# A six-layer decoder on one core: feed-forward rounding on GpSimd, maxima by four heads in one pass, gate products as scalar_tensor_tensor, new orders of work

## The reference

```python
x = _layernorm(x + _L0_attn_ref(x, Wq, Wk, Wv))                  # 16 heads of 16
x = _layernorm(x + _L0_xattn_ref(x, ctx, ctx, ...))              # 77 keys, biases
x = _layernorm(x + _L0_ffn_ref(x, w_gate, w_up, w_down))         # see below
x = _layernorm(x + _L1_attn_ref(x, qkv_w, ...))                  # rotary q and k
x = _layernorm(x + _L1_xattn_ref(ctx, x))                        # alignment by dynamic programming
x = _layernorm(x + _L1_ffn_ref(x, ...))                          # attention whose output is gated
```

## Time and profile before

| | us |
|---|---|
| median of three runs (6032.72 to 6035.66) | 6035.6 |
| the profiled execution | 6025.65 |
| its span, first to last instruction | 6023.9 |
| PE busy | 5378.2 (89%) |
| DVE busy | 4989.1 (83%) |
| ACT busy | 4263.0 (71%) |
| POOL busy | 2542.2 (42%) |

### The profile page before, as it was taken

How to read it: one execution, slowest core, us unless ns; L and a number is a source line. 1 busy time by engine, 2 the same in 40 slices (tenths; PEclk the granted TensorE clock), 3 DMA queues, 4 the chain that set the end, 5 groups by cost and what they waited for, 6 DMA issues and landing times. The chain is left out here.

```text
span 6023.9 us, 139116 instructions
## 1 busy us (share of the span) xinstructions
PE 5378.2 (89%) x54914; PEld 3756.3 (62%) x54914; DVE 4989.1 (83%) x11551; ACT 4263.0 (71%) x8049; POOL 2542.2 (42%) x2574
## 2 busy tenths in 40 slices
PE   6999999969999999977999999999309999999998
PEld 4666666646666666655777767767206666666666
DVE  6888888869999999986777777777678888888887
ACT  5777777758888888875666666666326777777776
POOL 0112111223333333333444444444107777777775
PEclk9999999989999999999999999999659999999999
DMA  1111111110000000001010010010100000000000
GB/s 53 49 43 45 47 43 49 40 32 29 30 29 26 30 30 30 25 24 34 29 33 29 29 33 29 29 33 29 39 26 18 26 30 26 30 26 30 26 30 22
DMA packets 140663, 193.91 MB, mean 32 GB/s; under 512 B 26353, under 2 KB 63985, under 8 KB 139633
## 3 DMA queue, kind: packets, MB, share of 16 engines
q1 hardware_dynamic: 140016, 185.00, 9.8%
HBM read 112.77 MB, written 72.18 MB: 31 GB/s over the span
## 5 line engine op out<-in xcount | busy, mean ns | idle before, releaser
L1193 DVE TENSOR_REDUCE Cmp<-pj 128x2 f32<-128x512 f32 x1024 | 635.7, 684 | 145.7 <-PE pj L874 145.6
L1193 DVE TENSOR_REDUCE Dmp<-pj 128x2 f32<-128x512 f32 x1024 | 649.0, 681 | 84.2 <-PE pj L874 84.0
L1013 ACT ACTIVATE Cpr<-pj 128x512 f32<-128x512 f32 x1024 | 528.9, 604 | 221.8 <-PE pj L807 221.8
L1193 DVE TENSOR_REDUCE Amp<-pj 128x2 f32<-128x512 f32 x1024 | 629.5, 682 | 65.0 <-PE pj L874 65.0
L1013 ACT ACTIVATE Apr<-pj 128x512 f32<-128x512 f32 x1024 | 522.0, 615 | 191.9 <-PE pj L807 191.9
L1013 ACT ACTIVATE Dpr<-pj 128x512 f32<-128x512 f32 x1024 | 526.5, 599 | 185.5 <-PE pj L807 185.4
L1127 POOL TENSOR_SCALAR Ave<-Amv 128x2 f32<-128x2 f32 x64 | 14.6, 228 | 976.9 <-DVE Amv L1261 976.9
L1127 POOL TENSOR_SCALAR Bve<-Bmv 128x2 f32<-128x2 f32 x128 | 29.2, 228 | 874.5 <-DVE Bmv L1261 874.5
L1099 POOL TENSOR_TENSOR Dnrm<-Dnrm,power 128x32 f32<-128x32 f32 x64 | 348.7, 5449 | 51.2 <-DVE Dnrm L1171 51.2
L807 PE MATMUL pj<-Dq,Dk 32*128 32x256 f32 x4096 | 332.8, 403 | 0.2 <-ACT Dpr L1013 0.2
L807 PE MATMUL pj<-Aq,Ak 32*128 32x256 f32 x4096 | 328.0, 396 | 2.1 <-DVE Aq L1200 1.2
(11 more groups left out here) (305 smaller groups left out, 14980.6 us busy)
## 6 DMA issues: line engine op xcount, KB each, us to landing
Ax0T<-in_xT SPq DMA_DIRECT2D x64, 256.0 KB, 2.9
Ax<-in_x SPq DMA_DIRECT2D x64, 256.0 KB, 3.1
x_A_scratch<-Ax SPq DMA_DIRECT2D x64, 256.0 KB, 2.0
Bx<-x_A_scratch SPq DMA_DIRECT2D x64, 256.0 KB, 2.9
x_B_scratch<-Bx SPq DMA_DIRECT2D x64, 256.0 KB, 2.0
Cx<-x_B_scratch SPq DMA_DIRECT2D x64, 256.0 KB, 2.8
x_C_scratch<-Cqr SPq DMA_DIRECT2D x64, 256.0 KB, 2.0
Dx<-x_C_scratch SPq DMA_DIRECT2D x64, 256.0 KB
```

Source lines behind the costliest of these rows:

```text
L1013: ck.tell(act.activation(dst, ck.bank(step + (bank,))[0:n, :], ACT.Exp, scale=HD ** -0.5), "probs_ready", step)
L1193: ins = dve.tensor_reduce(dst, src, AX.X, ALU.max, negate=True)
```

## The change

Five things change in the code, and with them the orders. `GROUPS` is 4 in A and B and stays 3 in C and D. A3's value bias is added by DVE when it writes the values, and ACT no longer copies them nor adds the bias behind the attention. A `max` step of pass C takes four heads, one in each row group, and four banks; the steps become half as many. The feed-forward input is rounded by POOL, with DVE keeping the scales. The gate products are all scalar_tensor_tensor, the first of them two instructions where it was one, with the factor 2 x 3 moved to another product.

```diff
-GROUPS = 3
+GROUPS = {"A": 4, "B": 4, "C": 3, "D": 3}
-VALUE_BIASES = ("A3_bv", "A4_bv")
+VALUE_BIASES = ("A4_bv",)
+VALUES_BY_ACT = ("A4",)
+ROW_GROUPS = {"A1": 2, "A2": 2, "A3": 4, "A4": 2}
 def max_heads(att, i):
+    n = ROW_GROUPS[att]
+    i, part = divmod(i, 4 // n)
+    groups = range(n * part, n * part + n)
     if tiles_of(att) == 2:
-        c, e, pair = i // 4, i % 4 // 2, i % 2
-        return [[8 * c + 2 * g + e] for g in (2 * pair, 2 * pair + 1)]
+        c, e = divmod(i, 2)
+        return [[8 * c + 2 * g + e] for g in groups]
...
-                        for i in range(2):
+                        for i in range(len(heads)):
                             ck.wait_bank_free(step + (i,))
                         for hh in range(len(heads[0])):
                             for t in range(QT):
-                                for i in range(2):
+                                for i in range(len(heads)):
...
+                    elif kind == "fq":          # gpsimd
+                        ck.wait("scales_ready", step)
+                        for t in range(QT):
+                            ins = pool.tensor_scalar(xq_f[s][:, t], x[s][:, t], qsc[s][:, t, 3:4], MAGIC, ALU.mult, ALU.add)
+                        link(ck, ins)
+                        ck.tell(pool.tensor_scalar(xq[s][:], xq_f[s][:], MAGIC, QMAX, ALU.subtract, ALU.min), "xq_ready", step)
...
-                        link(ck, dve.reciprocal(qsc[s][:, :, 2:3], qsc[s][:, :, 1:2]))
-                        link(ck, dve.tensor_scalar(qsc[s][:, :, 3:4], qsc[s][:, :, 2:3], QMAX, None, ALU.mult))
-                        for t in range(QT):
-                            ins = dve.tensor_scalar(xq_f[s][:, t], x[s][:, t], qsc[s][:, t, 3:4], MAGIC, ALU.mult, ALU.add)
-                        link(ck, ins)
-                        link(ck, dve.tensor_scalar(xq[s][:], xq_f[s][:], MAGIC, QMAX, ALU.subtract, ALU.min))
+                        dve.reciprocal(qsc[s][:, :, 2:3], qsc[s][:, :, 1:2])
...
-                        dve.tensor_tensor(gs[s][:, 7:9, :], ex[s][:, :, nr:H + 1].rearrange("p t i -> p i t"),
-                                          gs[s][:, 6:7, :].to_broadcast([P, 2, QT]), ALU.mult)
-                        link(ck, dve.tensor_tensor(gs[s][:, 9, :], gs[s][:, 4, :], gs[s][:, 5, :], ALU.mult))
-                        dve.tensor_tensor(gs[s][:, 10, :], gs[s][:, 7, :], gs[s][:, 8, :], ALU.add)
+                        for i in range(2):
+                            dve.scalar_tensor_tensor(out=gs[s][:, 7 + i, :], in0=ex[s][:, :, nr + i], scalar=1.0,
+                                                     in1=gs[s][:, 6, :], op0=ALU.mult, op1=ALU.mult)
+                        link(ck, dve.scalar_tensor_tensor(out=gs[s][:, 9, :], in0=gs[s][:, 4, :], scalar=2.0 * ROUTED,
+                                                          in1=gs[s][:, 5, :], op0=ALU.mult, op1=ALU.mult))
+                        dve.scalar_tensor_tensor(out=gs[s][:, 10, :], in0=gs[s][:, 7, :], scalar=1.0, in1=gs[s][:, 8, :],
+                                                 op0=ALU.mult, op1=ALU.add)
```

More of the change, by code:

```diff
@@ L128, in before_core @@
     if att == "A1":
-        steps = steps[:2] + maxima(att, b, 0)[:2] + steps[2:] + maxima(att, b, 0)[2:]
+        half = max_steps(att) // 4
+        steps = steps[:2] + maxima(att, b, 0)[:half] + steps[2:] + maxima(att, b, 0)[half:]
     else:
@@ L146, in core @@
     if tiles_of(att) == 2:
-        return p[:1] + second[:2] + p[1:2] + second[2:] + shifted + p[2:3] + first + p[3:] + last
+        return p[:1] + second[:len(second) // 2] + p[1:2] + second[len(second) // 2:] + shifted + p[2:3] + first + p[3:] + last
     return p[:1] + second + shifted + p[1:] + first + last
@@ L200 @@
         "sp": (
-            526, 0, 209,
+            309, 526, 0,
         ),
@@ L278, in bank_uses @@
     if kind == "max":
-        return [step + (0,), step + (1,)]
+        return [step + (g,) for g in range(ROW_GROUPS[step[1]])]
     if kind == "gu":
@@ L296, in signals @@
             "xqT": ["xqT_ready"], "gu": ["tanh_ready"], "hq": ["hid_rounded", "hq_ready"], "hT": ["hqT_ready"],
[L297 removed]
+            "mix": ["exps_ready"], "v": ["v_ready"] * (att in VALUES_BY_ACT),
         },
         "dve": {
[L300 removed]
+            "q": ["q_tokens"] * (att in ("A3", "A4")), "k": ["q_tokens"] * (att == "A3"), "v": ["v_ready"] * (att not in VALUES_BY_ACT),
             "rot": ["dve_step", "k_rotated"] if att == "A3" else ["norms2"],
[L302 removed]
+            "max": ["max_done"] * ROW_GROUPS.get(att, 0), "shift": ["q_shifted"] * 2,
             "norm": ["dve_step", "normed"] + ["x_used"] * (att == "A1" and step[-1] == 1),
             "oproj": ["proj_taken"], "path": ["dve_step", "path_ready"], "expand": ["x4_used"],
[L305 removed]
+            "down": ["down_taken"], "ln": ["dve_step", "var_ready"], "fq": ["dve_step"] * 3 + ["scales_ready"],
             "gu": ["gated", "hid_ready"], "hq": ["dve_step"] * 3 + ["scale_ready"], "dist": ["dist_ready"],
@@ L349, with __init__ @@
 class Counts:
-    def __init__(self, lines):
+    def __init__(self, lines, groups):
         self.at, self.total, self.bank, self.banks = {}, {x: 0 for x in SIGNALS}, {}, [0] * BANKS
@@ L371, in __init__ @@
             if step[0] == "core":
-                self.group[step] = len(cores) % GROUPS
-                if len(cores) >= GROUPS:
-                    _, att, b, p = cores[-GROUPS]
+                self.group[step] = len(cores) % groups
+                if len(cores) >= groups:
+                    _, att, b, p = cores[-groups]
                     self.freed_by[step] = ("pv", att, b, octet_of(att, p))
@@ L556, in __init__ @@
                 self.ve, self.rstd = each("ve", [P, QT, 2]), each("rstd", [P, QT, 2])
-                self.pr = [[sb(f"{phase}pr{i}_{g}", [P, QT, S], F32, where) for g in range(4)] for i in range(GROUPS)]
+                self.pr = [[sb(f"{phase}pr{i}_{g}", [P, QT, S], F32, where) for g in range(4)] for i in range(GROUPS[phase])]
                 if phase == "A":
@@ L1021, in do @@
                         ck.tell(ins, "out_taken", step)
-                    elif kind == "v" and att in ("A3", "A4"):
+                    elif kind == "v" and att in VALUES_BY_ACT:
                         ck.wait_bank_full(step)
@@ L1172, in do @@
                                   "norms2", step)
-                    elif kind == "v" and att in ("A1", "A2"):
+                    elif kind == "v" and att not in VALUES_BY_ACT:
                         ck.wait_bank_full(step)
@@ L1337, in do @@
                                                           in1=gs[s][:, 10, :], op0=ALU.mult, op1=ALU.mult))
-                        ck.tell(dve.tensor_tensor(gs[s][:, 15, :], gs[s][:, 11, :], gs[s][:, 12, :], ALU.add), "mixed", step)
+                        ck.tell(dve.scalar_tensor_tensor(out=gs[s][:, 15, :], in0=gs[s][:, 11, :], scalar=1.0, in1=gs[s][:, 12, :],
+                                                         op0=ALU.mult, op1=ALU.add), "mixed", step)
                 walk(dve, "dve", do)
@@ L1390, in _ @@
                                                                          in1=out3[:], op0=ALU.mult, op1=ALU.add))
-                counts = Counts(lines)
+                counts = Counts(lines, GROUPS[phase])
                 with ExitStack() as blocks:
```

62 lines of the change are left out of this document (31 added, 31 removed).

## The result

The changed kernel takes 5862.9 us at the median of four runs (5853.6 to 5864.4); the kernel before 6034.2 (6029.7 to 6035.7). The ratio is 0.9714, 95% interval 0.9697 to 0.9731: 171 us faster. The forecast was 5782, its range 5700 to 5890; the time lies in the range, but 81 us above the forecast and outside the likeliest case's own range of 5710 to 5850. The profiled execution has a span of 5862.6 us.

A forecast was written before the change was run, and what follows sets the result against it. DVE was taken to bound pass B, PE passes A, C and D. Terms 26 + 64 + 90 + 74 = 254 us off 6025.65 gave 5772, set at 5782 against the runs' median; range 5700 to 5890.

The forecast's parts named there:

- likeliest case: Whole kernel: the forecast of 5782 us holds, own range 5710 to 5850, chance 0.71.
- mechanism of B: Pass B: DVE is the bound, so moving the rounding to POOL takes 1.0 us off the period, 64 us in all.
- The operation that the trace did not show: Pass B: POOL's 128x512 tensor_scalar with bf16 out, rounding the feed-forward input, taken as 2.4 us.
- rival 3: Pass B: POOL's rounding, layernorm, store, load and PE's keys close a ring; kernel slower, 6089 us at z = 9; chance 0.03.
- the values' bank: Pass A: PE needs this bank one score step later, when DVE's copy is done; 0.4 us a sequence, 26 us.
- the wait at maxima 7: Pass A: PE's wait before the second half of maxima 7, 0.5 us a sequence, stays because DVE's order there is unchanged.
- I take 1.4 of the 2.5: Pass C: the new order removes 1.4 of 2.5 us of PE stall a period, 90 us in all.
- the next limit: Pass C: with banks free in time, DVE, at some 20 us of work and links, becomes what limits the period.
- rival 1: Passes A and C: the new orders give nothing, DVE being late in C; 5898 us, chance 0.14.
- I take it as free of the wait: Pass D: gate products as scalar_tensor_tensor do not wait for POOL's port; 1.0 us less 0.1 for the extra instruction.
- Rival 2: Pass D: the port holds scalar_tensor_tensor too, so the 0.9 us is lost; 5840 us, chance 0.08.
- takes both off the way: Pass D: moving gate products and path clears the way from maxima 2 to the shift; part of 1.15 us, 74 us.

## Why the prediction was right, and where it was not

**Direction, mechanism of B, untouched parts: right.** B was held by DVE, and its period fell by 1.19 us where 1.0 was taken (DVE's rows of `fq` were 1.12 and the links 0.1). The operation that the trace did not show, bounded by 1.2 and 5.45 us and taken as 2.4, cost 1.93; the two half-size ones, taken at 1.23 from the earlier trace rows, cost 0.48. The ring of rival 3 never came near: PE's wait for the load ahead of its keys was 0.5 us in the whole stretch. The alignment took 191 us, 190 before.

**A (26 us forecast, none got).** The steps given were right: the values' bank came free in time, the wait at maxima 7 stayed, the fourth group was free, and the median fell by 0.35 us where 0.4 was taken. That size was in part luck: the reason given was the values' bank alone, and without the layernorm's move only 0.12 us came. What failed is the part never priced: the layernorm behind the shift moves GpSimd's layernorm, SP's store and the load queued behind it, and a load that had just been in time was not. The prediction followed that chain for B only, as rival 3. Its price, 27 us in A and 27 in D (from the first to the last start of the table's instruction, 63 periods: 1131 to 1104 and 1402 to 1375 us with the stores moved), is 54 of the 81 us that were missed.

**C (90 us forecast, 42 got): the term was mis-sized, and not by its stalls.** "I take 1.4 of the 2.5": the order took 2.0 off score steps and maxima, more than that. But 1.2 of it came back in the steps that now stand elsewhere, shifts, transpositions and projections, and only 0.8 was kept; the "little over half" left no room for so much. Nor was DVE "the next limit": relieved of the values' copy (0.64 us of its 18.3 us busy a period) it changed nothing. The same run rules out rival 1's reason, DVE. That the maxima as such gain little was right.

**D (74 us forecast, 42 got; from first to last start 46, and 73 with the later stores): with those the sum comes out, by a wrong step and so by luck.** "I take it as free of the wait" is false. The evidence was L1233, 481 ns beside GpSimd's power function of 5.45 us; what it showed was that the power function did not hold it up, not that the form is exempt. The Trainium skill, "SBUF — State Buffer", "Who interferes with whom", has a VectorE instruction with two SBUF inputs contend with a GpSimd instruction that reads SBUF. For the new form beside a 128x512 tensor_tensor that is what the runs show (1162 and 1170 ns), and the prediction's reading of the rule, that the form by itself would gain nothing, came true (1.0008). Beside the power function they do not bear it out. Rival 2 had that mechanism right and its price, 58 us, wrong: the new place took the products away from GpSimd's 128x512 instruction, so the old form was as fast there. And "takes both off the way" was counted as a gain of the place by itself, which the old round refutes: there it costs 73 us.

The lower end of the range, 5700, is not the sum of the passes' upper bounds as the text has it: those add up to 385 us, which would be 5651.

**What is left open.** Which of the other moves in D's new round makes the place pay was not tried. A likely one is that PE sends shift 0 ahead of score step 3, which stood the other way round before: DVE's wait ahead of the shift's addition is 0.8 us in the version with later stores, 1.6 in the old round with the products moved. But the layernorm behind maxima 5, `path` ahead of the gate, and norms and transpositions in another turn came with it. Open is also what makes a step in C 0.1 us longer: the records show its start only, and whether the bank, the operand or the wake-up comes last there stays unsettled. As for the clock, what makes one idle of a microsecond be followed by a slow stretch and the next not is not shown.

## What to carry to other kernels

When a step that feeds a store moves later, follow the store through its queue to the next load, in every pass and not only where the queue looks full; compare the mean period with the median, for a few long sequences hide in a wait of 13 us. Stalls taken off a full engine can come back in its other steps: here 0.8 us of 2.0 was kept. Price a move in an order inside the round in which it will stand, and look first for the wait that the moved work fills: out of the stretch in which DVE waited for PE it cost 1.0 us, into such a stretch it was worth 2.0.

## What the runs showed of the hardware

- PE's granted clock fell to 0.50 for 3.4 us around the end of an idle of 0.75 to 1.69 us, eight times in the steady parts of A and D, and not once there when the late loads were gone. Such a stretch makes a wait of 1 us cost a sequence of A 3 us (20.1 to 20.8 against 17.46). It does not follow from the idle alone: in the kernel before with the gate products moved, PE waited 1.45 us in each of 55 sequences (4604 to 5940) and four stretches came; with the projection moved as well, three came in D (at 4873.7, 5232.1 and 5614.4) with no idle over 0.3 us in the 8 us before them.
- A scalar_tensor_tensor of two elements a partition with both inputs in SBUF waits for GpSimd's 128x512 tensor_tensor, up to 1162 ns against 158 at the median.
- Not every GpSimd instruction holds VectorE up. Beside the power function one of 77x256 did not wait (63 of 64 started inside it, 483 ns at most); 60 of the changed kernel's products at L1340 start inside the layernorm's small power function (128x2, 0.72 us) and take 145 to 151 ns; and of A's 128x512 additions of two SBUF tiles (L1230), 62 start inside a tensor_scalar of GpSimd (L1142, 1.23 us) and take 692 ns at the median, 792 at most.
- GpSimd's tensor_scalar has two prices: 128x256 took 476 ns with a scalar from a tile and a constant (L1148) and 1225 with two scalars from tiles (L1142); 128x512 with two constants and bf16 out took 1928. Whether the scalars or the operations (multiply and add against subtract and multiply) make the difference was not tried.
